# A gated attention and feed-forward block: the queries' projection as a phase of its own by Strassen's scheme

## The chip, the cores and the metric

The kernel runs on one core of one Trainium2 chip. The metric is the device time of one execution in microseconds (us). A change is told from no change on this kernel from about 0.3% on.

## The reference, cut to what matters

All is float32. `x` is 2048 tokens (32 x 64) of 512 values, the context has the same shape. Each block of 64 tokens attends to itself.

```python
xn = layernorm(x)
Q = (xn @ Wq.T)      # 8 groups of 4 heads of 128
K = (ctx @ Wk.T); V = (ctx @ Wv.T)      # 8 heads of 128
probs = softmax(causal(Q K^T * 128**-0.5))       # within each 64 tokens
x = x + tanh(g_xattn) * (probs V) @ Wd.T
w_eff = w * (su @ sv)                            # for gate, up, down; rank 4
d = silu(xn2 @ gate_eff.T) * (xn2 @ up_eff.T)    # xn2 = layernorm(x), 1792 columns
x = x + tanh(g_ffn) * d @ down_eff.T
```

## The kernel before

Every large product is done in three passes: each operand is split into a high part in float32r (a copy on ScalarE) and a low part (the rest, a subtraction on VectorE or GpSimd), and `three_pass` (L205) multiplies high by high, high by low and low by high into one bank of PSUM. The order of the work on each engine is written out by hand, with semaphores.

The kernel has three stages. In the first, eight chunks of 256 context tokens give keys and values, which go to scratches in DRAM; layernorm columns of x are transposed between them. One chunk is 96 matmuls of 256 columns and 48 of 512.

The second stage runs 64 units: 8 key heads (`h`) by 8 chunks of 256 tokens. Step i of TensorE does `queries(i)` (48 matmuls of 256 columns), `output(i - 2, 0)`, `prob_transposes(i - 1)`, `output(i - 2, 1)` (12 matmuls of 512 columns each), `effective(i - 1)` in the first 42 units, `weighted_values(i - 1)` and `scores(i)` (8 float32 matmuls of 64 columns). `weighted_values` (L488) takes the probabilities of two token blocks as float32r pairs, spread over all 128 rows: 4 products, each of the probabilities' high part (L496) and low part (L498) with a stationary tile that holds high values in one half of its rows and low values in the other. For it ScalarE runs `probs_hi` (four copies of 64 rows) and `values_hi`, VectorE `probs_lo` and `values_lo`.

`effective(m)` makes the effective weights of the feed-forward stage, 42 tiles: `split_lr` (five operations, on VectorE) splits the rank-4 factors `el` and `er`, one float32r matmul of 512 columns (L465) multiplies them, VectorE multiplies by `e_raw`, and the result goes to a scratch in DRAM. In the last units the second layernorm's columns are transposed as well.

The third stage is the feed-forward product: 7 pairs of tiles of 128 hidden columns by 4 chunks of 512 tokens, 72 matmuls of 512 columns for each of the 28.

Of the kernel before, what the change touches and what calls it, by code (L numbers as in the profile page):

```python
# [5 lines left out]
F32 = mybir.dt.float32  # L6
F32R = mybir.dt.float32r
# [3 lines left out]
ds = bass.ds  # L11
# [12 lines left out]
NORM = NU - NCH + 3  # L24
# [12 lines left out]

def bass_flamingo_gated_block(nc, x, ctx_t, g_xattn, g_ffn, w1, wq, wd, wf, sf_l, sf_r, out):

    with ExitStack() as es:
        def sb(name, shape, dt=F32, stack=es):
            return stack.enter_context(nc.sbuf_tensor(name, shape, dt))

        def sem(name):
            return es.enter_context(nc.semaphore(name))

        kd = nc.dram_tensor("k_scratch", [HKV, NCH, P, C], F32).ap()  # L60
        vd = nc.dram_tensor("v_scratch", [HKV, NCH, P, CT, DK], F32).ap()
        ed = nc.dram_tensor("ffn_eff_scratch", [NP, P, D], F32).ap()


        ident = sb("ident", [P, P])
        mask2 = sb("mask2", [P, 2, S])
        mask = sb("mask", [P, S])
        tg = sb("tg", [P, 2])
        graw = sb("graw", [P, 2])
        neg_half = sb("neg_half", [P, 2])  # L70
        bn = sb("bn", [P, 2, 6])
        mean = sb("mean", [P, 2])
        half_gap = sb("half_gap", [P, 2])
        veps = sb("veps", [P, 2])
        rstd = sb("rstd", [P, 2])
        xn = sb("xn", [P, 2, D])
        row_max = sb("row_max", [P, CB * G // 2])
        row_sum = sb("row_sum", [P, CB * G // 2])
        row_inv = sb("row_inv", [P, CB * G // 2])
        X = sb("X", [P, TT, D])  # L80
        pt_lo = sb("pt_lo", [P, 2, CT, G * S], F32R)
        xt_hi = sb("xt_hi", [P, KC, T], F32R)
        with ExitStack() as start:
            w1_raw = sb("w1_raw", [P, 2 * KC * 2, 512], F32, start)
        xt_lo = sb("xt_lo", [P, KC, T], F32R)

        with ExitStack() as one:
            wk_hi = sb("wk_hi", [P, HKV, KC, DK], F32R, one)
            wk_lo = sb("wk_lo", [P, HKV, KC, DK], F32R, one)
            wv_hi = sb("wv_hi", [P, 2, KC, 512], F32R, one)  # L90
            wv_lo = sb("wv_lo", [P, 2, KC, 512], F32R, one)
            c_raw = sb("c_raw", [P, KC, C], F32, one)
            c_hi = [sb(f"c_hi{p}", [P, KC, C], F32R, one) for p in range(2)]
            c_lo = [sb(f"c_lo{p}", [P, KC, C], F32R, one) for p in range(2)]
            k_st = sb("k_st", [P, HKV, C], F32, one)
            v_st = sb("v_st", [P, 2, 4, CT, DK], F32, one)


        with ExitStack() as two:
            wq_hi = sb("wq_hi", [P, G, KC, DK], F32R, two)  # L100
            wq_lo = sb("wq_lo", [P, G, KC, DK], F32R, two)
            wq_raw = sb("wq_raw", [P, G, KC, DK], F32, two)
            k_sb = sb("k_sb", [P, C], F32, two)
            v_raw = sb("v_raw", [P, 2, CT, DK], F32, two)
            q_sb = sb("q_sb", [P, CB, G, S], F32, two)
            prob = sb("prob", [P, CB * G // 2, S], F32, two)
            wd_hi = sb("wd_hi", [P, 2, G, D], F32R, two)
            wd_lo = sb("wd_lo", [P, 2, G, D], F32R, two)
            wd_raw = sb("wd_raw", [P, G, D], F32, two)
            e_raw = sb("e_raw", [P, D], F32, two)  # L110
            e_eff = sb("e_eff", [P, D], F32, two)
            el_raw = sb("el_raw", [P, P], F32, two)
            er_raw = sb("er_raw", [P, D], F32, two)
            el = sb("el", [P, P], F32R, two)
            er = sb("er", [P, D], F32R, two)

            pt_hh = sb("pt_hh", [P, 2, CT, G * S], F32R, two)
            v_hl = sb("v_hl", [P, 2, CT, DK], F32R, two)  # L120
            o_hi = sb("o_hi", [P, G, C], F32R, two)
            o_lo = sb("o_lo", [P, G, C], F32R, two)


        with ExitStack() as three:
            d_hi = [sb(f"d_hi{t}", [P, FC], F32R, three) for t in range(2)]
            d_lo = [sb(f"d_lo{t}", [P, FC], F32R, three) for t in range(2)]
            s_sb = [sb(f"s_sb{t}", [P, FC], F32, three) for t in range(2)]
            d_sb = [sb(f"d_sb{t}", [P, FC], F32, three) for t in range(2)]
            sb("over_attention", [P, 4, D], F32, three)  # L130
            sb("over_k_v_q_prob", [P, 9, C], F32, three)
            gu_hi = [sb(f"gu_hi{t}", [P, 2, KC, P], F32R, three) for t in range(2)]
            sb("over_wd_hi1", [P, G, D], F32, three)
            gu_lo = [sb(f"gu_lo{t}", [P, 2, KC, P], F32R, three) for t in range(2)]
            sb("over_wd_lo1", [P, G, D], F32, three)
            dn_hi = [sb(f"dn_hi{t}", [P, D], F32R, three) for t in range(2)]
            dn_lo = [sb(f"dn_lo{t}", [P, D], F32R, three) for t in range(2)]
            f_raw = [sb(f"f_raw{t}", [P, 3, D], F32, three) for t in range(1)]
            sb("over_attention_2", [P, 34, P], F32, three)
            f_raw.append(sb("f_raw1", [P, 3, D], F32, three))  # L140

        bank = [es.enter_context(nc.psum_tensor(f"bank{i}", [P, 512], F32)) for i in range(8)]

        d_x = sem("d_x")  # L150
        d_g = sem("d_g")
        W1_PARTS = [(0, 1), (1, 2)] + [(n, n + 2) for n in range(2, HKV + 2 * KC, 2)]
        d_w1 = [sem(f"d_w1_{n}") for n in range(len(W1_PARTS))]
        d_c0, a_c0, v_c0 = sem("d_c0"), sem("a_c0"), sem("v_c0")
        d_c = sem("d_c")
        d_ko = [sem(f"d_ko{n}") for n in range(4)]
        d_vo = [sem(f"d_vo{n}") for n in range(2)]
        d_k, d_v, d_wq, d_wd = sem("d_k"), sem("d_v"), sem("d_wq"), sem("d_wd")
        d_e, d_eo, d_lr = sem("d_e"), sem("d_eo"), sem("d_lr")
        d_f = [sem(f"d_f{t}") for t in range(2)]  # L160
        d_out = sem("d_out")
        g_const, g_pow = sem("g_const"), sem("g_pow")
        c_split = sem("c_split")
        g_wq, g_wd = sem("g_wq"), sem("g_wd")
        g_f = [sem(f"g_f{t}") for t in range(2)]
        v_const = sem("v_const")
        a_tanh, a_w1, a_chi, a_k, a_xt = sem("a_tanh"), sem("a_w1"), sem("a_chi"), sem("a_k"), sem("a_xt")
        v_wk, v_wvh, v_wv, v_v = sem("v_wk"), sem("v_wvh"), sem("v_wv"), sem("v_v")
# [15 lines left out]
        def w1_loaded(eng, n):  # L184

            eng.wait_ge(d_w1[n // 2 + 1 if n else 0], 16)
# [1008 lines left out]
```

## Time and profile before

| | |
|---|---|
| median of 3 runs | 1614.29 us (1610.86 to 1615.04) |
| the profiled execution, its own time | 1610.04 us |
| its span, first to last instruction | 1608.4 us |
| TensorE busy | 1592.5 us, 99% |
| VectorE, ScalarE, GpSimd busy | 939.1, 544.1, 179.7 us |

TensorE's instructions are pipelined: the duration of a matmul in the trace goes on while the next already streams. What one costs in a row of many is the distance between two starts, which the chain of work and the timeline show, and not its duration.

### The profile page before, as it was taken

The numbers are of one execution on the slowest core, as the hardware profiler recorded it, in microseconds if no ns is written. First come the engines' busy times: TensorE is split into PE (matmuls) and PEld (weight loads), VectorE is DVE, ScalarE is ACT, GpSimd is POOL, SyncE is SP. The second block draws the span as 40 slices with busy tenths as digits, with TensorE's granted clock in tenths as the row PEclk, the third lists the DMA queues.
The fourth block names the chain that finished last, engine by engine and source line by source line (L and its number), as shares of the span: only waits on it lengthen the run. The fifth ranks groups of instructions, "written<-read, shape, count | busy, mean of one in ns | idle before, by whom it ended". The sixth has DMA issues, their size and how long they took to land.

```text
span 1608.4 us, 29272 instructions
## 1 busy us (share of the span) xinstructions
PE 1592.5 (99%) x9738; PEld 1419.3 (88%) x9738; DVE 939.1 (58%) x1640; ACT 544.1 (34%) x942; POOL 179.7 (11%) x155
## 2 busy tenths in 40 slices
PE   8999999999999999999999999999999999999999
PEld 8899989999999999999999989989888888888887
DVE  4334387777877777777765655578733333333233
ACT  3112143443533444434534444443312212212121
POOL 1111110300300300300300201120001101001010
PEclk9999999999999999999999999999999999999999
DMA  8433442332332422322320200102001001010002
GB/s 287 145 114 109 152 137 85 95 120 87 122 104 80 138 92 83 132 85 93 132 79 29 79 22 29 29 20 68 1 0 40 2 37 39 0 39 20 20 26 79
DMA packets 84969, 122.66 MB, mean 76 GB/s; under 512 B 7760, under 2 KB 54096, under 8 KB 82896
## 3 DMA queue, kind: packets, MB, share of 16 engines
q1 hardware_dynamic: 82640, 105.54, 20.3%
q0 software_dynamic: 2304, 16.78, 2.9%
q8 instruction: 16, 0.26, 0.1%
q14 instruction: 9, 0.07, 0.0%
HBM read 90.31 MB, written 31.98 MB: 76 GB/s over the span
## 4 chain that ended last, share of the span: by engine, by line
PE 90%; issue 8%; DVE 1%; POOL 1%; ACT 0%; DMA 0%; POOLq 0%; SPq 0%; DVEq 0%; ACTq 0%
PE bank L205 69%; PE bank L598 9%; PE bank L512 6%; PE bank L496 2%; PE bank L498 2%; PE bank L470 2%; PE bank L465 1%; PE bank L245 1%; POOL gu_lo L1139 0%; DMA w_raw<-in_w 0%; POOL dn_lo L1144 0%; DVE X L1045 0%; POOL wd_lo L1113 0%; DVE d_lo L1039 0%; DVE d_sb L1035 0%
## 5 line engine op out<-in xcount | busy, mean ns | idle before, releaser
L205 PE MATMUL bank<-xt_hi,wq_hi 128*128 (+1 forms) x1024 | 294.9, 288 | 0.0
L205 PE MATMUL bank<-xt_hi,wq_lo 128*128 (+1 forms) x1024 | 289.7, 283 | 0.0
L205 PE MATMUL bank<-xt_lo,wq_hi 128*128 (+1 forms) x1024 | 289.7, 283 | 0.0
L205 PE MATMUL bank<-wd_hi,o_hi 128*128 (+1 forms) x512 | 207.1, 404 | 0.0
L205 PE MATMUL bank<-wd_lo,o_hi 128*128 (+1 forms) x512 | 200.7, 392 | 0.0
L205 PE MATMUL bank<-wd_hi,o_lo 128*128 (+1 forms) x512 | 200.2, 391 | 0.0
L205 PEld LDWEIGHTS bank<-xt_lo,wq_hi 128*128 128x128 f32 x1024 | 196.4, 192 | 0.0
L205 PEld LDWEIGHTS bank<-xt_hi,wq_hi 128*128 128x128 f32 x1024 | 196.2, 192 | 0.0
L205 PEld LDWEIGHTS bank<-xt_hi,wq_lo 128*128 128x128 f32 x1024 | 196.1, 192 | 0.0
L1035 DVE TENSOR_TENSOR d_sb<-bank,s_sb 128x512 f32<-128x512 f32 x56 | 38.7, 691 | 249.6 <-ACT s_sb L754 249.6
L205 PE MATMUL bank<-xt_hi,gu_hi 128*128 (+1 forms) x448 | 174.6, 390 | 0.0
L983 DVE SCALAR_TENSOR_TENSOR X<-bank,tg,X 128x512 f32 (+1 forms) x128 | 96.0, 750 | 134.5 <-PE bank L205 134.3
L205 PE MATMUL bank<-xt_hi,gu_lo 128*128 (+1 forms) x448 | 174.4, 389 | 0.0
L205 PE MATMUL bank<-xt_lo,gu_hi 128*128 (+1 forms) x448 | 174.3, 389 | 0.0
L754 ACT ACTIVATE s_sb<-bank 128x512 f32<-128x512 f32 x56 | 33.5, 598 | 307.4 <-PE bank L205 307.4
L512 PE MATMUL bank<-k_sb,q_sb 128*128 128x64 f32 x1024 | 121.5, 272 | 0.8 <-issue 0.8
L512 PEld LDWEIGHTS bank<-k_sb,q_sb 128*128 128x128 f32 x1024 | 120.0, 192 | 1.0 <-issue 1.0
L715 ACT ACTIVATE pt_hh<-bank 64x512 fp32r<-64x512 f32 x128 | 75.7, 591 | 122.2 <-PE bank L470 120.7
L1107 POOL TENSOR_TENSOR wq_lo<-wq_raw,wq_hi 128x512 fp32r<-128x512 f32 x32 | 42.6, 1364 | 657.0 <-ACT wq_hi L688 657.0
L205 PEld LDWEIGHTS bank<-wd_hi,o_lo 128*128 128x128 f32 x512 | 96.2, 188 | 22.0
L708 ACT ACTIVATE prob<-prob 128x512 f32<-128x512 f32 x64 | 40.5, 632 | 219.0 <-DVE prob L920 219.0
L205 PEld LDWEIGHTS bank<-wd_hi,o_hi 128*128 128x128 f32 x512 | 96.5, 188 | 16.6
(99 smaller groups left out, 3064.0 us busy)
## 6 DMA issues: line engine op xcount, KB each, us to landing
v_raw<-v_scratch SPq DMA_DIRECT2D x128, 128.0 KB, 2.7
er_raw<-in_sf_r SPq DMA_DIRECT2D x42, 256.0 KB, 2.6
e_raw<-in_wf SPq DMA_DIRECT2D x42, 256.0 KB, 2.7
ffn_eff_scratch<-e_eff SPq DMA_DIRECT2D x42, 256.0 KB, 2.0
f_raw<-ffn_eff_scratch SPq DMA_DIRECT2D x14, 768.0 KB, 4.4
k_scratch<-k_st SPq DMA_DIRECT2D x32, 256.0 KB, 4.0
v_scratch<-v_st SPq DMA_DIRECT2D x16, 512.0 KB, 2.8
k_sb<-k_scratch SPq DMA_DIRECT2D x64, 128.0 KB, 2.4
```

What stands on the lines that cost most here:

```text
L205: last = eng.matmul(to, a, b, start=(n == 0), stop=(n == len(terms) - 1))
L470: last = pe.transpose(bank[2][:, s * P:(s + 1) * P], prob[:, 2 * s:2 * s + 2, :].rearrange("p b k -> p (b k)"), ident[:, :])
L496: pe.matmul(bank[4 + b][:, t * 256:(t + 1) * 256], v_hl[:, b, t, :], pt_hh[:, b, t, :], start=True, stop=False)
L498: last = pe.matmul(bank[4 + b][:, t * 256:(t + 1) * 256], v_hl[:, b, t, :], pt_lo[:, b, t, :], start=False, stop=True)
L512: last = pe.matmul(bank[2][:, n * S:(n + 1) * S], q_sb[:, cb, 2 * e:2 * e + 2, :].rearrange("p e s -> p (e s)"), k_sb[:, cb * S:(cb + 1) * ...
L598: last = pe.matmul(bank[4 + n][:, :], a[t][:, n * P:(n + 1) * P], w[t][:, :], start=(t == 0 and q == 0), stop=(t == 1 and q == 2))
L708: a.activation(prob[:, :, :], prob[:, :, :], ACT.Exp, scale=SCALE).then_inc(a_exp, 1)
L715: a.activation(pt_hh[b * S:(b + 1) * S, b, :, :].rearrange("p t k -> p (t k)"), bank[2][b * S:(b + 1) * S, :], ACT.Copy).then_inc(a_pt, 1)
L754: a.activation(s_sb[t][:, :], bank[2 * t][:, :], ACT.Silu).then_inc(a_s, 1)
L983: v.scalar_tensor_tensor(at, bank[6 + t][:, :], tg[:, 0:1], at, ALU.mult, ALU.add).then_inc(v_y, 1)
L1035: v.tensor_tensor(d_sb[t][:, :], bank[2 * t + 1][:, :], s_sb[t][:, :], ALU.mult).then_inc(v_m, 1)
L1107: g.tensor_tensor(wq_lo[:, e, :, :], wq_raw[:, e, :, :], f32(wq_hi[:, e, :, :]), ALU.subtract).then_inc(g_wq, 1)
```

## The change

The queries' projection leaves the units and becomes a phase between the first stage and the units. It runs over 32 quads: 2 blocks of 1024 tokens by 16 pairs of heads. A quad multiplies a 2 by 2 block matrix of weights (2 heads by 2 halves of the 512 inputs) with a 2 by 2 block matrix of tokens (2 halves of the inputs by 2 halves of 512 tokens). Strassen's scheme in Winograd's form does that in seven products in place of eight, each of 6 matmuls of 512 columns. GpSimd forms the sums of the weights (`left_sums`) and of the tokens (`x_sums`), ScalarE and GpSimd split them (`left_hi`, `left_lo`, `x_hi`; VectorE `x_lo`), ScalarE and VectorE combine the products. The queries go to a new scratch `q_scratch` and are loaded again in each unit; x is read a second time for the residual.

The effective weights are made in the quads: one in each, and a second at the end of ten of them (`E_END`); their split is two copies on ScalarE (`lr_hi`) and three subtractions on VectorE (`lr_lo`). Four of the eight pairs of layernorm columns (`columns`) move into quads 2, 5, 8 and 11.

A unit's weighted values are 4 float32 matmuls of 256 columns, each on 64 rows of the array (rows 0 to 63 for block b = 0, rows 64 to 127 for b = 1, into banks 4 and 5 in turn). The splits of probabilities and values are gone. `probs_out` is one copy of 512 columns. The order of a step is `output(i - 2, 0)`, `prob_transposes(i - 1)`, `scores(i)`, `weighted_values(i - 1)`, `output(i - 2, 1)`. The second layernorm is applied on GpSimd. Keys, queries, values and the outputs' splits are double buffered, weights' loads are issued from SP's queue, and all loops are written out in full. The diff replaces nearly the whole file; this is its core (blank lines left out):

```diff
+    qd = nc.dram_tensor("q_scratch", [HKV, NCH, P, 2, CB, 2, S], F32).ap()
...
+    E_MID, E_END, count = {}, {}, 0
+    for q in range(NQ):
+        E_MID[q], count = count, count + 1
+        if q % 3 == 1 and len(E_END) < NP - NQ:
+            E_END[q], count = count, count + 1
...
+        def quad_dmas(q):
+            if q - 1 in E_END:
+                m = E_END[q - 1]
+                store_e(m)
+                load_e(m + 1)
+            m = E_MID[q]
...
+                load_lr(m + 1)
+            store_e(m)
+            if m + 1 < NP:
+                load_e(m + 1)
+            if q in E_END and E_END[q] + 1 < NP:
...
+            store_q(q)
...
+        def product(q, n, to, a, b, onto=False):
+            blk, p = q // NHP, q % 2
+            three_pass(bank[to][:, :],
+                       [((wa_hi[p][:, a, k, :], wa_lo[p][:, a, k, :]),
+                         (xc_hi[blk][:, b, k, :], xc_lo[blk][:, b, k, :])) for k in range(2)],
+                       start=not onto, onto=onto).then_inc(p_p[n], 1)
...
+        def quad(q):
+            pe.wait_ge(a_wa, 3 * (q + 1))
+            pe.wait_ge(g_wa, 3 * (q + 1))
+            pe.wait_ge(a_xhi, 4 * (q // NHP + 1))
+            pe.wait_ge(v_xlo, 4 * (q // NHP + 1))
+            if q:
+                pe.wait_ge(a_c11, q)
+            else:
+                pe.wait_ge(a_k, 4 * NCH)
+                pe.wait_ge(v_v, 4 * NCH)
+            product(q, 1, 0, 0, 0)
+            if q:
+                pe.wait_ge(v_t2, q)
+            product(q, 6, 1, 4, 4)
+            if q:
+                pe.wait_ge(v_c12, q)
+            product(q, 5, 2, 3, 3)
+            if q:
+                pe.wait_ge(v_c21, q)
+            product(q, 4, 3, 2, 6)
+            effective(E_MID[q])
+            pe.wait_ge(a_s1, q + 1)
+            product(q, 2, 0, 1, 1, onto=True)
+            pe.wait_ge(v_t1, q + 1)
+            product(q, 7, 1, 5, 5, onto=True)
+            pe.wait_ge(a_s5, q + 1)
+            product(q, 3, 2, 6, 2, onto=True)
+            if q in E_END:
+                effective(E_END[q])
...
+        def weighted_values(u):
+            pe.wait_ge(a_pt, u + 1)
...
+            for t in range(CT):
+                for b in range(2):
+                    rows = slice(b * S, (b + 1) * S)
+                    last = pe.matmul(bank[4 + b][:, t * 256:(t + 1) * 256], v_sb[u % 2][rows, t, :],
+                                     pt[rows, t, :], start=True, stop=True)
+            last.then_inc(p_o, 1)
...
+        for q in range(NQ - 1):
+            quad(q)
+        scores(0)
+        quad(NQ - 1)
...
+            if i >= 2:
+                output(i - 2, 0)
+            if i <= NU:
+                prob_transposes(i - 1)
+            if i < NU:
+                scores(i)
...
+            if i <= NU:
+                weighted_values(i - 1)
+            if i >= 2:
+                output(i - 2, 1)
...
+        def left_hi(q):
+            p = q % 2
+            a.wait_ge(d_wq[p], 16 * (q // 2 + 1))
+            if q >= 2:
+                a.wait_ge(p_p[3], q - 1)
+            if q == 1:
+                a.wait_ge(p_v, 4 * NCH)
+            a.activation(wa_hi[p][:, 0:2, :, :].rearrange("p n k d -> p (n k d)"), wq_raw[p][:, 0, :],
+                         ACT.Copy).then_inc(a_wa, 1)
+            a.activation(wa_hi[p][:, 2, :, :].rearrange("p k d -> p (k d)"), wq_raw[p][:, 1, D // 2:],
+                         ACT.Copy).then_inc(a_wa, 1)
+            a.wait_ge(g_s, 4 * (q + 1))
+            a.activation(wa_hi[p][:, 3:7, :, :], ws[p][:, :, :, :], ACT.Copy).then_inc(a_wa, 1)
+        def lr_hi(m):
+            a.wait_ge(d_lr, 32 * (m + 1))
+            if m:
+                a.wait_ge(p_e, m)
+            a.activation(el[:, :], el_raw[:, :], ACT.Copy).then_inc(a_lr, 1)
+            a.activation(er[:, :], er_raw[:, :], ACT.Copy).then_inc(a_lr, 1)
...
+        def quad(q):
+            if q + 1 < NQ:
+                left_hi(q + 1)
+            a.wait_ge(p_p[1], q + 1)
+            if q:
+                a.wait_ge(v_t2, q)
+            a.activation(s1[:, :], bank[0][:, :], ACT.Copy).then_inc(a_s1, 1)
+            lr_hi(E_MID[q])
+            a.wait_ge(p_p[5], q + 1)
+            if q:
+                a.wait_ge(v_c22, q)
+            else:
+                for n in range(2):
+                    a.wait_ge(d_vo[n], 16 * NCH)
...
+            a.wait_ge(p_p[2], q + 1)
+            if q >= 2:
+                a.wait_ge(d_qo[q % 2], 16 * (q // 2))
+            a.activation(q_st[q % 2][:, :, 0:2, 0, :], bank[0][:, :].rearrange("p (n c s) -> p n c s", n=4, c=2),
+                         ACT.Copy).then_inc(a_c11, 1)
...
+        def lr_lo(m):
+            v.wait_ge(a_lr, 2 * (m + 1))
+            for to, raw, part in ((el, el_raw, slice(32, 64)), (el, el_raw, slice(96, 128)),
+                                  (er, er_raw, slice(64, 128))):
+                v.tensor_tensor(to[part, :], raw[part, :], f32(to[part, :]), ALU.subtract).then_inc(v_lr, 1)
...
+        def quad(q):
+            def split(ap):
+                return ap.rearrange("p (n c s) -> p n c s", n=4, c=2)
+            if q == 0:
+                for n in range(2):
+                    v.wait_ge(d_vo[n], 16 * NCH)
+            else:
+                v.wait_ge(v_c12, q)
+            v.wait_ge(p_p[6], q + 1)
+            v.wait_ge(a_s1, q + 1)
+            v.tensor_tensor(t1[:, :], bank[1][:, :], s1[:, :], ALU.add).then_inc(v_t1, 1)
+            if q - 1 in E_END:
+                effective(E_END[q - 1])
+            lr_lo(E_MID[q])
+            if q in STATS:
+                stats1(STATS[q])
+            effective(E_MID[q])
...
+            if q in E_END:
+                lr_lo(E_END[q])
+            if q in X_LO:
+                x_lo(X_LO[q])
+            v.wait_ge(p_p[7], q + 1)
+            if q:
+                v.wait_ge(v_c21, q)
+            v.tensor_tensor(t2[:, :], bank[1][:, :], s1[:, :], ALU.add).then_inc(v_t2, 1)
+            v.wait_ge(v_t2, q + 1)
+            v.wait_ge(a_s5, q + 1)
+            if q >= 2:
+                v.wait_ge(d_qo[q % 2], 16 * (q // 2))
+            to = q_st[q % 2]
+            v.tensor_tensor(to[:, :, 2:4, 1, :], split(t2[:, :]), split(s5[:, :]), ALU.add).then_inc(v_c22, 1)
+            v.wait_ge(p_p[4], q + 1)
+            v.tensor_tensor(to[:, :, 0:2, 1, :], split(t2[:, :]), split(bank[3][:, :]),
+                            ALU.subtract).then_inc(v_c21, 1)
+            v.wait_ge(p_p[3], q + 1)
+            v.tensor_tensor(to[:, :, 2:4, 0, :], split(bank[2][:, :]), split(t1[:, :]), ALU.add).then_inc(v_c12, 1)
...
...
+                for n in range(2):
+                    g.wait_ge(d_vo[n], 16 * NCH)
+            a11, a12 = wq_raw[p][:, 0, :D // 2], wq_raw[p][:, 0, D // 2:]
+            a21, a22 = wq_raw[p][:, 1, :D // 2], wq_raw[p][:, 1, D // 2:]
+            to = [ws[p][:, n, :, :].rearrange("p k d -> p (k d)") for n in range(4)]
+            g.tensor_tensor(to[0], a21, a22, ALU.add).then_inc(g_s, 1)
+            g.tensor_tensor(to[2], a11, a21, ALU.subtract).then_inc(g_s, 1)
+            g.wait_ge(g_s, 4 * q + 1)
+            g.tensor_tensor(to[1], to[0], a11, ALU.subtract).then_inc(g_s, 1)
+            g.wait_ge(g_s, 4 * q + 3)
+            g.tensor_tensor(to[3], a12, to[1], ALU.subtract).then_inc(g_s, 1)
+        def left_lo(q):
+            p = q % 2
+            raws = (wq_raw[p][:, 0, :], wq_raw[p][:, 1, D // 2:], ws[p][:, :, :, :].rearrange("p n k d -> p (n k d)"))
+            for n, (part, raw) in enumerate(zip((slice(0, 2), slice(2, 3), slice(3, 7)), raws)):
+                g.wait_ge(a_wa, 3 * q + n + 1)
+                g.tensor_tensor(wa_lo[p][:, part, :, :].rearrange("p n k d -> p (n k d)"), raw,
+                                f32(wa_hi[p][:, part, :, :]).rearrange("p n k d -> p (n k d)"),
+                                ALU.subtract).then_inc(g_wa, 1)
```

## Rows read from the trace of the kernel before

**Rows 1.** The page: TensorE's busy time; the granted clock in 40 slices

```profile
PE 1592.5 (99%) x9738; PEld 1419.3 (88%) x9738; DVE 939.1 (58%) x1640; ACT 544.1 (34%) x942; POOL 179.7 (11%) x155
...
PEclk9999999999999999999999999999999999999999
```

**Rows 2.** Windows: length, busy PE, PEld, DVE, ACT, POOL; clock, DMA share, GB/s

```profile
6.40:199.20 192.80, 192.78 (x1250) 177.47 (x1251) 76.78 (x145) 39.29 (x65) 27.79 (x20) 1.00 0.47 159
199.20:230.00 30.80, 27.42 (x206) 25.43 (x205) 25.55 (x52) 15.71 (x29) 6.83 (x7) 1.00 0.48 161
230.00:820.00 590.00, 590.00 (x4064) 543.72 (x4064) 459.63 (x806) 252.28 (x442) 60.58 (x50) 1.00 0.32 102
...
1166.00:1599.00 433.00, 432.82 (x1910) 358.31 (x1910) 144.64 (x215) 83.40 (x141) 46.96 (x36) 1.00 0.07 24
```

**Rows 3.** The chain of work through one unit with effective weights: start, us, what

```profile
230.64 8.55 PE bank L205 x60
239.19 0.44 PE bank L470 x4
239.63 2.77 PE bank L205 x12
242.40 0.23 PE bank L465
...
243.57 1.73 PE bank L512 x16
245.31 8.55 PE bank L205 x60
```

**Rows 4.** The same chain: starts of two units in a row, without effective weights

```profile
847.30 8.56 PE bank L205 x60
861.96 8.56 PE bank L205 x60
```

**Rows 5.** Timeline of TensorE: the first matmul of `queries`, and the first after it

```profile
700.34 0.36 PE L205 MATMUL bank<-xt_hi,wq_hi 128*128 x1
...
706.17 0.40 PE L205 MATMUL bank<-wd_hi,o_hi 128*128 x1
```

**Rows 6.** The chain: a chunk of keys and values; products of the third stage

```profile
89.28 22.43 PE bank L205 x144
...
1169.34 5.44 PE bank L205 x24
1174.78 2.72 PE bank L598 x12
```

**Rows 7.** Groups by form, TensorE: matmuls of L496, weight loads of L512 (count, us, mean ns)

```profile
L496 PE MATMUL bank<-pt_hh,v_hl 128*128 128x256 f32 x256 | 65.4, 289 | 1.1 <-issue 0.8 <-ACT pt_hh L719 0.3
...
L512 PEld LDWEIGHTS bank<-k_sb,q_sb 128*128 128x128 f32 x1024 | 120.0, 192 | 1.0 <-issue 1.0
```

**Rows 8.** Groups by form, VectorE

```profile
L951 DVE TENSOR_TENSOR er<-er_raw,er 32x512 fp32r<-32x512 f32 x84 | 63.0, 750 | 2.6
...
L914 DVE TENSOR_TENSOR prob<-bank,mask 128x512 f32<-128x512 f32 x64 | 43.4, 677 | 1.4 <-issue 1.2
...
L951 DVE TENSOR_TENSOR el<-el_raw,el 64x128 fp32r<-64x128 f32 x42 | 12.1, 289 | 1.4
```

**Rows 9.** Groups by form, ScalarE and GpSimd

```profile
L688 ACT ACTIVATE wq_hi<-wq_raw 128x512 fp32r<-128x512 f32 x32 | 17.5, 622 | 7.0 <-DMA wq_raw<-in_wq 7.0
...
L638 ACT ACTIVATE c_hi<-c_raw 128x1024 fp32r<-128x1024 f32 x7 | 7.4, 1061 | 61.3 <-PE bank L205 61.2
...
L1107 POOL TENSOR_TENSOR wq_lo<-wq_raw,wq_hi 128x512 fp32r<-128x512 f32 x32 | 42.6, 1364 | 657.0 <-ACT wq_hi L688 657.0
...
L1082 POOL TENSOR_TENSOR c_lo<-c_raw,c_hi 128x1024 fp32r<-128x1024 f32 x7 | 16.8, 2399 | 38.6 <-ACT c_hi L638 38.6
```

**Rows 10.** DMA issues: what, count, KB each, median us to landing

```profile
er_raw<-in_sf_r SPq DMA_DIRECT2D x42, 256.0 KB, 2.6
...
v_scratch<-v_st SPq DMA_DIRECT2D x16, 512.0 KB, 2.8
```

More of the change, by code:

```diff
@@ L23 @@
 NU = HKV * NCH
-NORM = NU - NCH + 3
 I = 1792
@@ L77, in bass_flamingo_gated_block @@
[L77 to L96, printed above, removed]
@@ L192, in f32 @@
-        def f32(ap):
-            return ap.bitcast(F32)
-        def three_pass(eng, to, pairs, waits=()):
-            terms = [t for (ah, al), (bh, bl) in pairs for t in ((ah, bh), (ah, bl), (al, bh))]
-            for n, (a, b) in enumerate(terms):
-                for pair, semaphore, value in waits:
-                    if n == 3 * pair:
-                        eng.wait_ge(semaphore, value)
-                last = eng.matmul(to, a, b, start=(n == 0), stop=(n == len(terms) - 1))
-            return last
@@ new lines, in normalised @@
+        def normalised(u):
+            v.wait_ge(a_exp, u + 1)
+            v.tensor_reduce(row_sum[:, :], prob[:, :, :], AX.X, ALU.add).then_inc(v_sum, 1)
+            v.wait_ge(v_sum, u + 1)
+            v.reciprocal(row_inv[:, :], row_sum[:, :]).then_inc(v_inv, 1)
+            v.wait_ge(v_inv, u + 1)
+            v.tensor_tensor(prob[:, :, :], prob[:, :, :],
+                            row_inv[:, :].rearrange("p (n o) -> p n o", o=1).broadcast_to(rows),
+                            ALU.mult).then_inc(v_p, 1)
@@ new lines, in _ @@
+        for n in range(2 * KC):
+            half, k = n // KC, n % KC
+            v.wait_ge(d_w1[(HKV + n) // 2 + 1], 16)
+            v.tensor_copy(wv_hi[:, half, k, :], w1_raw[:, HKV + n, :]).then_inc(v_wvh, 1)
+            v.wait_ge(v_wvh, n + 1)
+            v.tensor_tensor(wv_lo[:, half, k, :], w1_raw[:, HKV + n, :], f32(wv_hi[:, half, k, :]),
+                            ALU.subtract).then_inc(v_wv, 1)
+        for c in range(NCH):
+            values_out(c)
+            if 3 <= c <= 6:
+                x_lo(c - 3)
+            if 2 <= c <= 5:
+                stats1(c - 2)
+                apply1(c - 2)
@@ new lines, in _ @@
+        for q in range(NQ):
+            quad(q)
+            if q == NQ - 2:
+                masked_minus_max(0)
+        v.wait_ge(a_tanh, 1)
+        normalised(0)
+        for i in range(1, NU + 2):
+            if 59 <= i:
+                stats2(i - 59)
+            if i >= 2:
+                add_to_x(i - 2, 0)
+            if i < NU:
+                masked_minus_max(i)
+            if i <= NU:
+                out_lo(i - 1)
+            if i < NU:
+                normalised(i)
+            if 60 <= i:
+                columns2_lo(i - 60, (2, 3))
+            if i >= 2:
+                add_to_x(i - 2, 1)
```

1713 lines of the change are left out of this document (824 added, 889 removed).

## The prediction

> **What bounds the kernel now.** I read the page first: TensorE is busy for 99% of the span and its clock is granted in full in all 40 slices [rows 1]. At 2.4 GHz, the upper level, throughout, there is nothing to gain from the clock. The windows say where it is less dense [rows 2]: from 230 to 820 us it is busy for 590.00 of 590.00, in keys and values and in the third stage nearly so too, and only the passage between the first stage and the units has a gap, 3.4 us of 30.8. So the time is the sum of TensorE's instructions at their distances, plus what the change makes it wait. DMA moves 102 to 161 GB/s at a busy share of 0.32 to 0.48; VectorE is busy in the units for 78% of the time.
>
> The distances come from the chain. The third stage spends 5.44 us on 24 matmuls of 512 columns and 2.72 on 12: 0.2267 each [rows 6]. A chunk of keys and values takes 22.43 us; less 48 x 0.2267 that leaves 0.120 for each of its 96 matmuls of 256 columns. So half the columns cost more than half the time. A unit lasts 14.67 us (230.64 to 245.31): 8.55 for queries and the first half of the output, 0.44 for transposes, 2.77 for the other half, 0.23 for the effective weight, 1.73 for scores (16 records for 8 calls), and what is left, 0.94, for the 8 matmuls of the weighted values, 0.118 each [rows 3]. The queries alone, from their first matmul to the output's first, take 5.83 us [rows 5].
>
> **Queries: removed and added.** Removed are 64 x 5.83 = 373.1 us. Added are 32 quads x 7 products x 6 = 1344 matmuls of 512 columns at 0.2267: 304.7 us. That is 68.4 less: one product in eight by the scheme, the rest because 512 columns go out at a time. The 42 effective weights still cost 0.23 each, and the eight pairs of columns are still transposed; they only move.
>
> **The units without them.** A unit of before less queries, effective weight and weighted values is 14.67 - 5.83 - 0.23 - 0.94 = 7.67 us. The new unit is 7.67 + W, W the new weighted values. Beside it lies VectorE: five operations of 512 columns for the softmax, two splits of the output and two additions to X, nine at about 0.7 (0.68 in [rows 8]) and a small one, some 6.5 us, under the 7.67 + W. The splits that leave VectorE and ScalarE are worth nothing by themselves, since TensorE covers them. In step i, scores end at 4.9 us, the weighted values follow, ScalarE and VectorE split them by about 3.0 us after their end, while `output(i - 2, 1)` takes 2.76 and the next step's first output needs the split a little later still; the softmax of the next unit is done some 1.5 us before its transposes are due. I count no wait in the steady units. Units without effective weight last 14.66 us, not 14.44 [rows 4]: 0.2 us of waiting for the probabilities' copies, in 16 units, which goes: 3 us less. The 3.4 us of the passage go as well.
>
> **W, the unknown.** No matmul of before works on 64 rows, and no float32 one on 256 columns. Before, a unit had eight records of 0.118. The scores show float32: two records a call, 1.73 / 16 = 0.108 each though they stream 64 columns, each with its load of 128 x 128 weights [rows 3, 7]. Four calls make eight records. Lower end: they cost what the scores' records cost, 0.86 us. Upper end: the scores' records are bound by their columns, and four times as many cost four times as much, 3.46. Between them: the kernel's own three passes leave out only low by low, so a full float32 product has four such terms; two records then carry two each, 2 x 256 columns, and the row for 512 columns is 0.2267: 1.81 us in series. The Trainium skill, "FP8 and Floating Point Precision", TensorE Precision Notes, gives true FP32 four passes, which agrees with that count; no row of before separates it from the ends.
>
> But calls of b = 0 and b = 1 alternate, use different halves of the array's rows and write different banks. If a matmul can stream in one half while the one before it streams in the other, then of the records A1 A2 B1 B2 C1 C2 D1 D2 the pairs A2 B1, B2 C1 and C2 D1 run together, and in order that makes five slots: 5 x 0.2267 = 1.13. Rows can't show it; that the array already takes weights for the next matmul while one streams (88% busy loads beside 99% busy matmuls [rows 1]) speaks for independent parts. I take 1.13 and keep 0.86 and 3.46 as ends. The skill's "TensorE: Matmul & The Clock Gate", Part 3, says that matmuls in distinct row groups run concurrently without more ado, with four groups of 32 rows measured at 3.07 times; by that W is about the 1.13, and without it the 1.81. Nothing here shows which.
>
> **Waits that the quads add.** A product is 1.36 us; a regular quad is p1 0, p6 1.36, p5 2.72, p4 4.08, effective 5.44, p2 5.67, p7 7.03, p3 8.39, end 9.75. A result is usable some 0.17 us after the next start (0.40 of duration less 0.23 of distance [rows 5, 6]). *First quad.* TensorE first waits until the last values are copied out of banks 2 and 3, 0.9 us. `left_sums(1)` on GpSimd waits for the last store of values (512 KB, 2.8 us to landing [rows 10]) and takes four sums of 256 columns at 0.8 (an estimate from 1.36 for 512 and 2.40 for 1024 [rows 9]): 6.3 us. ScalarE's `left_hi(1)` stands ahead of the copy s1 and waits for it, plus 1.06; s1, `lr_hi` 0.9 and `lr_lo` 1.35 (0.29 twice and 0.70 [rows 8]) follow: the effective matmul starts at 10.4 instead of 5.44. 5.0 us. *Regular quads.* ScalarE: `left_hi` to 2.34, s1 to 2.97, `lr_hi` to 3.95; VectorE `lr_lo` to 5.33: ready just as TensorE comes. VectorE's five combinations of 0.69 and the rest are 6 of 9.98 us; GpSimd's three splits and four sums 7.8; both fit. *The ten quads with a second effective weight.* Its factors are loaded once `lr_lo` of the first is done (5.35), the second DMA half a microsecond later, 2.6 to landing: 8.5. `lr_hi` to 9.4, `lr_lo` to 10.8, TensorE due at 9.75 goes at 10.9: 1.2. Behind it waits the next load, and VectorE's product: the next quad's effective matmul is late by another 0.36, with `x_hi` ahead on ScalarE in four of them 0.8. Together 17.3 us. *Into the units.* Combinations end 1.7 us after the last product, `normalised(0)` takes 1.6, and then the first output waits behind scores(1), weighted values and their splits, with nothing else to do: 6.0. Sum 29.2.
>
> **Hidden.** Of keys and values nothing changes on TensorE. The larger load on ScalarE, VectorE and GpSimd there (`x_hi`, `x_lo`, sums) fits in 22 us a chunk. Loads of a unit, 512 KB in 8.8 us, are issued two units ahead. At the end stats and low parts of the second layernorm put some 10.9 us on VectorE against 9.7 on TensorE for seven units; the slack of 1.5 us and the later ones take it. The third stage is as before.
>
> **The sum**, against the profiled execution's own 1610.0: - 68.4 - 3 - 3.4 + 29.2 + 64 x (1.13 - 0.94) = + 12.2, gives 1576.6. The runs shown have a median 0.26% above it (1614.29 / 1610.04): **1581 us**.
>
> **Rivals.**
> *The halves run in series.* W = 1.81 adds 43.5: 1620, as a median 1624. Slower, by one mechanism. It decides from W = 1.65 on, where 64 x (W - 0.94) uses up the 45.6 that all else brings. For it: no row shows two matmuls streaming at once.
> *A drain at each change of shape.* If going to 64 rows and back each costs the tail of a matmul (0.289 of duration less 0.118 of distance [rows 7, 3], 0.17), 2 x 64 x 0.17 = 22 us: 1603. The skill's "TensorEngine Tiling (Array Packing)", Key Properties, says that a change of tiling mode drains TensorE, which speaks against the change; the trace has no such change to test it.
> *The quads starve.* A quad moves 1 MB of queries, 0.5 of weights and 0.77 of effective weights in 9.8 us, 235 GB/s, against 159 at share 0.47 before [rows 2]: about 0.7 busy. If factors land late or the engines' chain slips by 1 us a quad, 32 us: 1613.
> *Float32 is bound by columns*, W = 3.46: 1730.
> *All goes well*: W = 0.86 and no late factors: 1546 to 1562.
>
> **Chances.** As forecast 0.47; drains 0.10; starved quads 0.11; series 0.25; bound by columns 0.03; better than all 0.04. About 0.3% is what can be told from no change here, 1609.4 to 1619.1. Faster: 0.47 + 0.10 + 0.04, half of the starved (0.05) and the part of series where my waits are too high (0.03), 0.69. Same: 0.04 + 0.07 = 0.11. Slower: 0.02 + 0.15 + 0.03 = 0.20. The forecast case alone spans 1563 to 1596; the range must take in most of series: 1562 to 1631.
>
> **What would show it.** Quads 9.8 to 10 us apart, with waits for `lr_lo` at each second effective weight; the first quad some 15 us; units 8.8 us apart (9.5 if in series), the weighted values' b = 0 and b = 1 records starting together or not. I am wrong if W is not 1.13, if the engines beside TensorE pace the quads, or if straight-line code is fetched too slowly.

## The result, and the profile after

The changed kernel takes 1670.35 us (median of 4 runs, 1664.38 to 1673.41), the kernel before 1612.57 in the same measurement: a ratio of 1.035, 95% interval 1.032 to 1.039. It is slower, by more than the range allowed. The profiled execution took 1664.38 us, with a span of 1662.6.

The page: busy time, clock, and the 40 slices of TensorE ([rows 1] of before).

```profile
PE 1575.3 (95%) x8010; PEld 1308.6 (79%) x8010; DVE 908.8 (55%) x1436; ACT 464.9 (28%) x810; POOL 425.9 (26%) x378
...
PE   8999898888889889999999999998999999999999
...
PEclk9999999999999989999999999998999999999999
```

TensorE is busy 17 us less than before and the span is 54 us longer. The thin part is slices 5 to 15, the quads. The windows show it ([rows 2] of before; columns the same):

```profile
194.60:592.00 397.40, 334.47 (x1362) 262.48 (x1363) 251.62 (x363) 152.68 (x282) 257.84 (x241) 0.95 0.67 229
592.00:620.00 28.00, 23.03 (x110) 18.64 (x110) 16.21 (x27) 5.83 (x11) 0.00 (x0) 0.85 0.58 201
620.00:1040.00 420.00, 420.00 (x2446) 350.85 (x2446) 298.29 (x470) 121.39 (x212) 31.00 (x24) 1.00 0.31 102
```

From 620 to 1040 us, in the units, TensorE has no gap and the full clock. In the quads it is idle for 63 us of 397, and the mean granted clock is 0.95. What it waited for (total us, times, longest):

```profile
PE bank L471 <- DVE er L916: 56.0, 27, 5.8
PE bank L566 <- POOL xn L1172: 6.9, 2, 6.0
PE bank L399 <- DVE wk_lo L1052: 6.3, 1, 6.3
PE bank L399 <- DVE t L952: 3.4, 2, 2.2
PE bank L399 <- DVE q_st L963: 3.2, 3, 1.6
PE bank L527 <- DVE prob L987: 2.9, 1, 2.9
```

L471 is the effective matmul, L916 `lr_lo`. 27 waits of 56.0 us, where the prediction had 21 (the first quad's and two for each second effective weight) of 22.3 us. A steady unit in the chain ([rows 3] of before):

```profile
625.15 5.69 PE bank L399 x24
630.84 0.44 PE bank L527 x4
631.28 1.73 PE bank L513 x16
633.01 1.06 PE bank L542 x8
634.08 5.67 PE bank L399 x24
```

The unit is 8.93 us here, 8.91 as a rule; the weighted values are the 1.06. VectorE's groups in the quads (count, us, mean ns, idle time before):

```profile
L916 DVE TENSOR_TENSOR el<-el_raw,el 32x128 fp32r<-32x128 f32 x84 | 63.3, 753 | 32.2 <-ACT er L701 29.9
L916 DVE TENSOR_TENSOR er<-er_raw,er 64x512 fp32r<-64x512 f32 x42 | 38.4, 915 | 1.3
...
L958 DVE TENSOR_TENSOR q_st<-t,s 128x512 f32<-128x512 f32 x31 | 27.6, 890 | 1.1
L936 DVE TENSOR_TENSOR t<-bank,s 128x512 f32<-128x512 f32 x32 | 22.1, 692 | 54.8 <-PE bank L399 30.4 <-ACT s L709 24.2
L952 DVE TENSOR_TENSOR t<-bank,s 128x512 f32<-128x512 f32 x32 | 22.1, 689 | 24.1 <-PE bank L399 23.7
L963 DVE TENSOR_TENSOR q_st<-bank,t 128x512 f32<-128x512 f32 x31 | 21.1, 680 | 0.0
```

The reader is to see two things. The subtraction on `el`, 32 rows by 128, takes 0.75 us on average, where [rows 8] has 0.29 for 64 rows. And of four additions of the same size, those that read one operand from PSUM (`bank`) take 0.68 to 0.69, and the one that reads both from SBUF (`t`, `s`) takes 0.89.

### The profile page after: what moved, and what is told of

Read it like the earlier page. It is cut to its first block, busy times and chain, and to the rows that moved or that the text cites. A ratio compares the mean times of both kernels' runs of the same rounds, so it can differ in the third digit from the quotient of the medians.

```text
span 1662.6 us, 20957 instructions
## 1 busy us (share of the span) xinstructions
PE 1575.3 (95%) x8010; PEld 1308.6 (79%) x8010; DVE 908.8 (55%) x1436; ACT 464.9 (28%) x810; POOL 425.9 (26%) x378
## 3 DMA queue, kind: packets, MB, share of 16 engines
q8 instruction: 65, 1.06, 0.3%
## 4 chain that ended last, share of the span: by engine, by line
PE 84%; DVE 7%; DMA 3%; POOL 3%; issue 2%; ACT 1%; SPq 0%; DVEq 0%; ACTq 0%; POOLq 0%
PE bank L399 61%; PE bank L618 9%; PE bank L513 7%; PE bank L542 4%; DVE el L916 3%; DVE er L916 2%; PE bank L527 2%; DMA e_raw<-in_wf 1%; PE bank L471 1%; DMA er_raw<-in_sf_r 1%; DMA c_raw<-in_ctx_t 1%; DVE t L936 1%; DMA k_scratch<-k_st 1%; PE bank L566 0%; PE bank L445 0%
## 5 line engine op out<-in xcount | busy, mean ns | idle before, releaser
L399 PE MATMUL bank<-wd_hi,o_hi 128*128 128x512 f32 x512 | 208.7, 408 | 2.1 <-ACT o_hi L755 2.1
L399 PE MATMUL bank<-wd_hi,o_lo 128*128 128x512 f32 x512 | 201.4, 393 | 0.0
L399 PE MATMUL bank<-wd_lo,o_hi 128*128 128x512 f32 x512 | 201.0, 393 | 0.0
L399 PE MATMUL bank<-xc_hi,wa_hi 128*128 128x512 f32 x448 | 182.5, 407 | 7.5 <-DVE t L952 3.4
L399 PE MATMUL bank<-xc_lo,wa_hi 128*128 128x512 f32 x448 | 181.2, 404 | 0.0
L399 PE MATMUL bank<-xc_hi,wa_lo 128*128 128x512 f32 x448 | 180.9, 404 | 0.0
L399 PE MATMUL bank<-xt_hi,gu_hi 128*128 128x512 f32 x448 | 174.5, 389 | 0.0
L399 PE MATMUL bank<-xt_hi,gu_lo 128*128 128x512 f32 x448 | 174.3, 389 | 0.0
L399 PE MATMUL bank<-xt_lo,gu_hi 128*128 128x512 f32 x448 | 174.3, 389 | 0.0
L1009 DVE SCALAR_TENSOR_TENSOR X<-bank,tg,X 128x512 f32<-128x512 f32 x128 | 95.5, 746 | 61.2 <-PE bank L399 61.2
L399 PEld LDWEIGHTS bank<-wd_lo,o_hi 128*128 128x128 f32 x512 | 97.2, 190 | 18.3
```

Source lines behind the costliest of these rows:

```text
L399: last = pe.matmul(to, a, b, start=(start and n == 0), stop=(stop and n == 3 * len(pairs) - 1), skip_group_check=onto)
L1009: v.scalar_tensor_tensor(to, bank[t][:, :], tg[:, 0:1], to, ALU.mult, ALU.add).then_inc(v_y, 1)
```

## The experiments

Each starts from the changed kernel unless it says otherwise. The kernel before ran beside them at 1611.61 us (e1 to e4), 1610.77 (e5 to e8), 1610.54 (e9, e10) and 1612.82 (e11). e6, e7 and e8 were timed over several rounds; the others are one time and one profile. The four executions of the changed kernel differ by 9 us, with mean clocks of 0.982 for the profiled one, the shortest, and 0.975 to 0.976 for the others; so where single times lie within some 10 us of each other I go by waits and clock. "Less" and "more" are against the profiled execution.

### e1: no effective weights

```diff
-            effective(E_MID[q])
             pe.wait_ge(a_s1, q + 1)
...
-            lr_hi(E_MID[q])
...
-            lr_lo(E_MID[q])
```

and the same for the second ones, the loads and the store.

> Leaves out the effective weights altogether (loads, splits, product, store; the third stage reads the raw weights). Theory A, the quads wait for the splits of the rank-4 factors (56 us of TensorE's waits in the changed kernel, and a lower clock behind them): the 32 quads take 9.6 to 10 us each, the whole kernel 1575 to 1590 us. Theory B, GpSimd's and ScalarE's chain of sums and splits of Wq, or the DMA, paces the quads whatever they wait for: a quad still takes over 11.5 us, the kernel 1635 us or more.

Measured 1565.17 us, 99 less than the changed kernel's profiled execution, and 10 below the lower end that I had for theory A. The phase:

```profile
194.60:506.50 311.90, 309.84 (x1390) 256.79 (x1391) 140.07 (x208) 125.51 (x205) 255.75 (x241) 1.00 0.52 184
```

A quad is 9.75 us with the same sums, splits and stores of queries, and the clock is granted in full. Theory A holds: the chain of sums and splits of Wq does not pace the quads. The 42 matmuls themselves would cost 9.7 us, so 89 of the 99 are what comes with them.

### e2: no subtractions on the factors

```diff
-            lr_lo(E_MID[q])
...
-            if q in E_END:
-                lr_lo(E_END[q])
```

> Leaves out only the three subtractions of lr_lo on VectorE; loads, copies, product and store of the effective weights stay. If the subtractions (held up behind GpSimd) are most of the wait: TensorE's wait ahead of the effective matmul falls from 56 to under 20 us and the time to 1615 to 1630. If the factors' late landing is most of it: the wait stays at 35 us or more and the time is over 1640.

The load of the next factors waits for the two copies here, since the subtractions are gone, so it is issued sooner too. Measured 1601.09 us, 63 less, lower than I expected; the wait ahead of the effective matmul is 8.2 us. The three subtractions, with the earlier load, are the larger part; loads, copies, matmuls and the multiplication that stay cost 36 us against e1.

### e3: GpSimd without the low parts of Wq

```diff
-            if q + 1 < NQ:
+            if q + 1 < 2:
                 left_lo(q + 1)
```

> GpSimd makes the low parts of Wq only for the first two quads (the later ones multiply by those); everything else stays. If VectorE's operations that read and write SBUF alone wait for GpSimd's: the mean of the el subtractions falls from 0.75 us to under 0.5 and that of q_st from t and s from 0.89 to about 0.75, the wait ahead of the effective matmul from 56 to about 35 us, the time to about 1635. If VectorE's durations have another cause (DMA writes to SBUF): they stay at 0.75 and 0.89, and the time moves by under 5 us.

Measured 1640.36 us. VectorE's groups over the kernel:

```profile
L918 DVE TENSOR_TENSOR er<-er_raw,er 64x512 fp32r<-64x512 f32 x42 | 35.4, 844 | 1.3
L918 DVE TENSOR_TENSOR el<-el_raw,el 32x128 fp32r<-32x128 f32 x84 | 35.1, 417 | 37.4 <-ACT er L703 35.1
L960 DVE TENSOR_TENSOR q_st<-t,s 128x512 f32<-128x512 f32 x32 | 23.5, 735 | 1.1
```

0.75 fell to 0.42, 0.89 to 0.74, and `er` from 0.92 to 0.84 (GpSimd still forms the sums). The wait fell from 56 to 40.7 us, near what I expected for this cause. VectorE's operations with both inputs in SBUF are held up by GpSimd's; that they wait for its end is read from the timeline in e10.

### e4: both blocks' weighted values from the same rows

```diff
-                    rows = slice(b * S, (b + 1) * S)
+                    rows = slice(0, S)
```

> The weighted values of both token blocks are taken from rows 0 to 63 (so block 1 gets block 0's). If matmuls in different halves of the array's rows run beside each other: the eight records take 1.8 us in place of 1.06, a unit 9.65 in place of 8.91, the kernel 1664 + 48 = 1712. If the eight records are cheap for another reason: no change.

Measured 1727.43 us. The chain:

```profile
707.39 0.44 PE bank L527 x4
707.82 1.73 PE bank L513 x16
709.56 1.92 PE bank L542 x8
711.48 5.69 PE bank L399 x24
```

1.92 in place of 1.06, 0.24 a record. 64 x 0.86 = 55 us more of the 63. Another 6 lie in the quads, whose code is the same: 418 us in place of 412, at a clock of 0.93 in place of 0.95. The same quads differ by that much from one execution to the next. The halves of the array do run beside each other, and in series it would be nearly the 1.81 of the prediction.

### e5: the weights' sums ahead of the tokens'

```diff
+            if q + 2 < NQ:
+                left_sums(q + 2)
             if q in COLUMNS:
                 x_sums(COLUMNS[q])
-            if q + 2 < NQ:
-                left_sums(q + 2)
```

> The changed kernel with GpSimd's left_sums ahead of x_sums in the four quads that have both (3, 6, 9, 12). If part of the quads' loss is GpSimd's order (the weights' sums, ScalarE's left_hi and the copy s1 queue behind 3.3 us of x_sums): those four quads shorten by about 3 us each, the kernel 1650 us. If only the factors' splits count: less than 4 us.

Measured 1651.67 us, 12.7 less. In the changed kernel's chain `x_sums`, `left_sums`, `left_hi` and s1 stand one behind the other there, and TensorE's next effective matmul, in quads 4, 7 and 10, waits 5.4 us each time, in quad 13 2.9; here these four wait 1.8 each, 12 us less. But other waits grow, and all of them in the quads fall by 2 us only, from 63.5 to 61.2. The larger part is the clock, over the quads:

```profile
194.60:594.30 399.70, 339.22 (x1434) 264.69 (x1434) 261.78 (x377) 156.77 (x289) 262.44 (x241) 0.99 0.69 233
```

0.99 in place of 0.95. After the waits of 5.4 us the changed kernel ran 6.8 us at the lower level, and such waits are gone. So the 12.7 are not a price of `x_sums` alone. The prediction has no term for `x_sums` in the quads: its 7.8 us for GpSimd are three splits and four sums.

### e6: the effective weights in the units

```diff
             if i <= NU:
                 weighted_values(i - 1)
+            if i <= NP:
+                effective(i - 1)
...
                 add_to_x(i - 2, 0)
+            if i <= NP:
+                lr_lo(i - 1)
             if i < NU:
                 masked_minus_max(i)
...
                 normalised(i)
+            if i <= NP:
+                effective(i - 1)
```

`lr_hi(i)` follows the exponentials on ScalarE, and the loads and the store go out in the units.

> Strassen's quads and float32 weighted values as in the changed kernel, but the effective weights are made in the first 42 units, as before: splits on ScalarE and VectorE between the first addition to X and the mask, the product after the weighted values in bank 3, the multiplication after the softmax. Theory: the place was the fault, since GpSimd rests in the units and VectorE has 2.6 us a unit to spare: quads as without effective weights, 42 x 0.23 = 10 us more than that run, 1575 us, 2.3% faster than before. Rival: VectorE's 8.3 us of work in 9.1 makes the softmax or the factors late by 1 us a unit: 1615 us or more.

Measured 1576.03 us, ratio to before 0.979 (0.977 to 0.980). The same subtractions of `el` and `er`, now with GpSimd at rest:

```profile
L914 DVE TENSOR_TENSOR el<-el_raw,el 32x128 fp32r<-32x128 f32 x84 | 30.3, 361 | 3.5 <-ACT er L698 0.9
L914 DVE TENSOR_TENSOR er<-er_raw,er 64x512 fp32r<-64x512 f32 x42 | 28.9, 689 | 1.3
```

TensorE never waits for them. It costs 11 us more than e1, of which 9.7 are the matmuls, and the quads take 312 us as in e1. The place was the fault.

### e7: as e6, with e5's order and another place for ws1

```diff
-    ws = [at(143, "ws0", [P, 4, 2, DK]), at(201, "ws1", [P, 4, 2, DK])]
+    ws = [at(143, "ws0", [P, 4, 2, DK]), at(19, "ws1", [P, 4, 2, DK])]
```

> As e6_effective_in_units, with the weights' sums ahead of x_sums, and the second buffer of weight sums (ws1) where nothing of the first stage lies, so that the first quad doesn't wait for the last stores of values. The 2.1 us that TensorE waits for the copy s1 in the first quad without effective weights go: 1573 us. If it costs or gives anything else by the moved buffer: outside 1570 to 1578.

Measured 1572.77 us, ratio to before 0.977 (0.975 to 0.978): the fastest kernel of this study, 3 us under e6, of which the removed wait for s1 (2.0 us in e6's trace) is the larger part. What is left for e5's order is 1 us: without the effective weights in the quads TensorE has no wait that it could remove.

### e8: the kernel before, with float32 weighted values alone

```diff
-                        pe.matmul(bank[4 + b][:, t * 256:(t + 1) * 256], v_hl[:, b, t, :], pt_hh[:, b, t, :],
-                                  start=True, stop=False)
-                        last = pe.matmul(bank[4 + b][:, t * 256:(t + 1) * 256], v_hl[:, b, t, :],
-                                         pt_lo[:, b, t, :], start=False, stop=True)
+                        rows = slice(b * S, (b + 1) * S)
+                        last = pe.matmul(bank[4 + b][:, t * 256:(t + 1) * 256], v_raw[rows, t, :],
+                                         pt[rows, t, :], start=True, stop=True)
```

and the splits of both operands are gone.

> The kernel before with one part of the change alone: the weighted values as 4 float32 matmuls on 64 rows each, no splits of probabilities and values. The unit grows by 1.06 - 0.94 = 0.12 us, less 0.2 in the 16 units that waited for copies: +5 us, within 0.3% to 0.4% of before. If the float32 form brings a wait or a drain in this order of work, +20 us (1633); if the relief of ScalarE and VectorE is worth more than that, faster than before.

Measured 1628.19 us, ratio 1.011 (1.009 to 1.012): 17 us more than before, where I expected 5, and near the 20 of the other case. The chain of a unit:

```profile
602.79 2.77 PE bank L207 x12
605.56 0.23 PE bank L466
605.79 1.06 PE bank L499 x8
606.85 1.93 PE bank L513 x16
608.78 8.55 PE bank L207 x60
```

The same 16 records of the scores take 1.93 us behind the half-row matmuls, 1.73 in [rows 3]. So 64 x (0.12 + 0.20) = 20 us less the 3 of the copies is what was measured. The chain goes by ends, which are modelled, and puts all of the 0.20 behind the half rows. By the starts it divides: from the effective matmul to the first half-row one it is 0.32 us instead of 0.23, and from the first score to the next product's start 1.81 instead of 1.70. So going to 64 rows and back costs 0.20 us together, about half of it each way. The rival with drains had 0.17 each way; that it is a drain is not shown.

### e9: a quarter of the queries' store

```diff
-            sp.dma_start(qd[g, 4 * b:4 * b + 4, :, ep].rearrange("a p c e s -> p a (c e s)"),
+            sp.dma_start(qd[g, 4 * b:4 * b + 1, :, ep].rearrange("a p c e s -> p a (c e s)"),
```

The units load the first chunk's queries for all four.

> The changed kernel, but each quad stores only the queries of its first chunk (256 KB in place of 1 MB) and the units load that chunk's for all four. If the DMA load makes the factors land late and so part of TensorE's wait: the wait of ScalarE's el copy for er_raw (68 us in the phase) falls by a third or more, TensorE's wait ahead of the effective matmul from 56 to under 48 us, the time to under 1650. If the landing is late only because it is issued late (after lr_lo of the tile before): both stay, 1658 to 1668.

Measured 1665.75 us. The phase moves 168 GB/s in place of 227 and nothing else changes: ScalarE's wait for `er_raw` 66 us against 68, TensorE's 58 against 56. So the load of the stores on the DMA is no cause.

### e10: without the ten second effective weights

```diff
-        if q % 3 == 1 and len(E_END) < NP - NQ:
+        if False:
```

> The changed kernel without the second effective weights of ten quads (32 of 42 tiles are made, the third stage reads ten groups of them again). By the working of the prediction these ten cost 17.3 us of waiting and 2.3 of matmuls: about 1643. If they are the larger part of the loss (the other 22 quads run freely): 1620 or less. If every quad waits for its own factors as well: the ten take under a third of the 99 us that all effective weights cost, 1635 to 1650, with 30 us of waits left.

None of the three: 1679.03 us, slower with less work, though in one execution only. All waits in the quads are what they were, 64.6 us against 63.5; 63.7 of them stand ahead of the effective matmul. What grew is the time at the lower clock, a mean of 0.90 from 194.6 to 605 us in place of 0.95. Many quads are alike now, and one can be read from the timeline:

```profile
402.62 2.42 POOL L1158 TENSOR_TENSOR wa_lo<-ws,wa_hi 128x1024 fp32r<-128x1024 f32 x1
402.69 0.69 DVE L936 TENSOR_TENSOR t<-bank,s 128x512 f32<-128x512 f32 x1 [1.56 <-PE bank L399]
403.41 2.51 DVE L916 TENSOR_TENSOR el<-el_raw,el 32x128 fp32r<-32x128 f32 x2
405.95 1.10 DVE L916 TENSOR_TENSOR er<-er_raw,er 64x512 fp32r<-64x512 f32 x1
407.11 0.50 PE L471 MATMUL bank<-er,el 128*128 128x512 f32 x1 [1.79 <-DVE er L916]
...
407.45 0.40 PE L399 MATMUL bank<-xc_hi,wa_hi 128*128 128x512 f32 x1
...
408.25 0.63 PE L399 MATMUL bank<-xc_hi,wa_hi 128*128 128x512 f32 x1
408.68 0.63 PE L399 MATMUL bank<-xc_lo,wa_hi 128*128 128x512 f32 x1
...
411.24 0.50 PE L399 MATMUL bank<-xc_lo,wa_hi 128*128 128x512 f32 x1
411.57 0.39 PE L399 MATMUL bank<-xc_hi,wa_lo 128*128 128x512 f32 x1
```

The addition from PSUM (L936) runs its 0.69 us beside GpSimd's subtraction of 1024 columns. The next one, on `el`, is held until that ends at 405.04: the first of the two ends at 405.18. The changed kernel's trace has 26 such subtractions of `el` that begin within that GpSimd instruction, 0.5 to 1.7 us after its start, and every one ends 0.14 to 0.15 us after its end. `lr_lo` takes 3.64 us in place of 1.35, TensorE comes at 405.15 and idles until 407.11. Up to there the forecast is right: it has `lr_lo` begin 3.95 us after the quad's first matmul, and here it is 3.7. Then the second cost: the starts lie 0.43 us apart instead of 0.23, TensorE runs at its lower level, 1.2 GHz, for some eight matmuls (granted clock 0.50 from 408.3 to 411.2 us). The windows of two quads, each from one effective matmul to the next:

```profile
393.66:407.11 13.45, 11.66 (x44) 9.10 (x44) 9.55 (x10) 4.29 (x8) 7.69 (x8) 0.87 0.55 183
472.79:484.65 11.86, 10.06 (x44) 7.99 (x44) 7.55 (x9) 4.29 (x8) 7.71 (x8) 1.00 0.93 289
```

Both do the same 9.75 us of work, with a wait of 1.8 us before it and after it. In the first the clock falls behind the wait, in the second it doesn't, and the fall costs the difference, 1.6 us. Of e10's 21 waits of 1.8 to 2.1 us, 15 are followed by a fall within 2 us and 6 are not; what decides it the runs don't show. From quad to quad the subtractions meet GpSimd's longest instruction again. That the waiting itself keeps the engines in step, and that the second effective weights had disturbed it, is a reading of this trace that no run tests.

The changed kernel's own trace agrees that the second effective weights, which I had blamed, are not what was missed: its waits ahead of the ten second matmuls are 2.7 us together, those in the quads right behind 12.4, in sum less than the 17.3 forecast. The other 41 are ahead of the first effective matmuls of the other quads, where the forecast had the 5.0 of the first quad.

### e11: the quad's own split first

```diff
+            lr_hi(E_MID[q])
             if q + 1 < NQ:
                 left_hi(q + 1)
...
+            lr_lo(E_MID[q])
             v.wait_ge(p_p[6], q + 1)
             v.wait_ge(a_s1, q + 1)
```

> The changed kernel with the same work, but the split of a quad's own factors comes first: lr_hi ahead of left_hi on ScalarE, lr_lo (and the pending multiplication) ahead of t1 on VectorE. Theory: the loss is that the 3.6 us of subtractions start 3 us into the quad and end 1.8 us after they are due, and each such wait lets the clock fall for some eight matmuls. Started 2 us sooner they are in time: waits ahead of the effective matmul under 25 us in place of 56, the time 1600 to 1630. Rival: the quad is too full for these engines (or the factors land too late), and the wait only moves to t1, s1 or the weights: 1650 or more.

Measured 1645.14 us, 19 less, between the two cases that I expected. The wait ahead of the effective matmul halves, to 27.4 us, but those ahead of the products (for `t` and `q_st`) grow from 6.6 to 15.9, and ScalarE waits 124 us, not 68, for factors that are not there yet. `er` now meets GpSimd's long instruction (463.14 + 2.44 = 465.58, and 0.55 us later it is done):

```profile
463.14 2.44 POOL L1158 TENSOR_TENSOR wa_lo<-ws,wa_hi 128x1024 fp32r<-128x1024 f32 x1
463.36 2.77 DVE L916 TENSOR_TENSOR er<-er_raw,er 64x512 fp32r<-64x512 f32 x1
```

So this order alone does not cure it, with the factors single buffered and GpSimd at work for 7.7 us of each quad.

## Why the prediction was wrong

**The step that failed** is "Regular quads ... VectorE `lr_lo` to 5.33: ready just as TensorE comes". It took the durations of [rows 8] from units where GpSimd mostly rests and put them beside 7.8 us of GpSimd's work that the same paragraph had counted. In that company `lr_lo` takes up to 3.6 us in place of 1.35. (The 0.70 for `er` in it is 0.75 in [rows 8]; that is no part of the miss.) The step had 0.1 us of slack, so nearly the whole excess fell on TensorE. The second failure is that its waits were priced at their own length, with no term for the clock behind them.

The Trainium skill has the rule that I did not apply: "SBUF — State Buffer", Who interferes with whom, says that a VectorE instruction with two SBUF inputs contends with a GpSimd instruction that reads SBUF, and that the one that comes second blocks until the other is done. The traces here agree: 0.89 against 0.69 for the same addition, 2.51 for two that take 0.29 each, the release at the end of GpSimd's instruction. With the 2.40 us of GpSimd's 1024 columns [rows 9] `lr_lo` could be held up to that long in each quad. Half of it in each of the 32 quads, an estimate, is 38 us and would have brought the forecast from 1576.6 to 1615, no faster than before.

**The amount.** The 32 quads and scores(0) lasted from 194.6 to 605.4 us, 410.8. My sum for them was 304.7 + 9.7 + 3.5 of columns + 1.7 of scores + 23.2 of waits (29.2 less the 6.0 into the units) = 342.8. The 68 us more are: waits of 63.5 us (56.0 + 3.4 + 3.2 + 0.9) in place of 23.2, 40; and TensorE busy for 347.5 us in 194.6 to 605 where its work is 319.6, 28. Of these some 18 are the lower clock behind the waits: a mean of 0.95 over 411 us is 41 us at half speed, in 4 of which TensorE was idle anyway. The rest is what each of the 33 waits costs beyond its row, 0.17 us of the last matmul's tail and 0.11 more before the second one behind it. I had a term for neither. The prediction said "there is nothing to gain from the clock" and did not ask what the waits that it added would lose.

**Point by point.**
- Queries: 1344 matmuls at 0.2267, right: e1's phase is 311.9 us with them, columns and gaps, at a clock of 1.00.
- W: 1.13 forecast, 1.06 measured; by e4 for the reason given (1.92 in series). The rival with drains was right in part: by e8 the two changes of shape cost 0.20 a unit, some 13 us, where it had 22 and the forecast nothing. The unit is 8.91 against 8.80: W was 0.07 too high, which hides part of that. That is luck.
- First quad: 0.9 and 5.0 forecast, 0.88 and 5.76 measured, by the chain described. Into the units: 6.0 forecast, 2.9 + 2.1 measured.
- The ten second effective weights: 17.3 us forecast as the main cost. The changed kernel has 15 there, and 41 in the other quads; e10, without the second ones, waits as long.
- `x_sums` in four quads: not in the forecast; 12 us of waits in the quads behind them by e5, of which only 2 are gained on balance, and a higher clock in that one execution.
- The starved quads as a rival: it had 32 us from late factors or engines that slip by 1 us a quad. e9 excludes the load of the stores; engines did slip, but the rival doesn't name what made them. e2 leaves 36 us against e1: 9.7 of matmuls, 15 more of waits in the quads, and the rest clock (0.98 against 1.00) and restarts.
- Second layernorm on GpSimd: hidden by the forecast; TensorE waits 6.9 us for `xn`, 6.0 of them once, at the second pair of its columns: in the chain GpSimd's splits of the third stage's weights, 7.5 us, stand ahead of it.
- Together 68 in the quads, 7 in the units, 7 there, 2 of waits for key copies in the first stage, less 1 of the passage: 83 of the 88 us between 1576.6 and 1664.4. Behind the waits into the units and for `xn` the granted clock was 0.50 for 10.2 us each (611.8 to 622.0 and 1154.5 to 1164.7), with TensorE busy for 8.1 and 7.1 of them. That is some 4 us each, again without a term; with it the list is 3 us over, which I have not traced.
- By parts: against before, the quads and the new units without effective weights gain 46 us (e1), with them in the units 35 (e6); float32 weighted values alone lose 17 (e8). They also relieve VectorE, but whether e6's place needs that was not run: Strassen's quads with the weighted values of before are untested and could be the faster kernel.

Open is which of ScalarE's copies, the factors' single buffer and the multiplication causes the 15 us of waits between e2 and e1; a second buffer for the factors found no room in SBUF during the quads and was not tried.

## What to carry to other kernels

Before moving work to another phase, lay it beside what the *other* engines do there: a duration holds for the company that it was measured in, and VectorE's two-input operations from SBUF are held by GpSimd's. Price a wait on TensorE at its length plus what the clock may then lose: in e10 a wait of 1.8 us cost 1.6 more in most quads and nothing more in some, and over the changed kernel's quads 63 us of waits cost some 18 more by the clock. And when less work makes a kernel slower, or an edit gains more than its waits, look at the granted clock of the stage before you name a cause.

## What the runs showed of the hardware

- VectorE with both inputs in SBUF waits until GpSimd's running instruction has ended (0.29 us becomes up to 2.0 in the changed kernel's chain); with one input in PSUM it doesn't (0.69 beside it, in e10).
- Float32 matmuls of 64 rows in alternate halves of the array and alternate banks: 8 records of 256 columns in 1.06 us, in the same half 1.92 (e4). Going to 64 rows and back costs 0.20 us together (e8 against before).
- After idle stretches of 1.8 to 2.1 us in otherwise dense work the granted clock fell to 1.2 GHz within 2 us in 15 cases of e10 and stayed at 2.4 GHz in 6. A fall lasted some eight matmuls of 512 columns and cost 1.6 us.
